# Causal attention with a recurrence behind it: from trips of 128 queries of two batches to trips of 64 queries of four

## The reference

```python
q, k, v = split(x @ c_attn_w + b)                       # heads of 32
k_img, v_img = cond @ uk_w.T + uk_b, cond @ uv_w.T + uv_b   # one key and value per batch
scores = q @ [k_img, k].T / sqrt(32)                    # [8, 16, 512, 513]
scores = where(key <= query + 1, scores, -10000) + mask
x1 = x + softmax(scores) @ [v_img, v] @ c_proj_w + b_proj
xw = x1 @ Wx + b_h
h_t = tanh(h_(t-1) @ Wh + xw_t)                         # t = 0 .. 511, h_(-1) = cond
out = x1 + h
```

## Time and profile before

| | |
|---|---|
| median of three runs | 1697.04 us (1691.76 to 1697.95) |
| profiled execution | 1689.44 us |
| its span | 1687.6 us |
| TensorE (PE) busy, of the span | 1521.2 us |
| setup, before the first unit's scores | 0 to 48 us |
| four blocks of attention | 48 to 246, 617, 1014 and 1425 us |
| tail, 128 steps | 1445 to 1678 us |

### The profile page before, as it was taken

One profiled execution on the slowest core, in us unless ns is written; L12 is line 12 of the kernel. 1 busy time (PEld: TensorE's weight loads), 2 busy tenths in 40 slices (PEclk: granted clock), 3 DMA queues, 4 the chain that ended last, 5 costly groups with the idle time before them and its releaser, 6 DMA issues.

```text
span 1687.6 us, 65682 instructions
## 1 busy us (share of the span) xinstructions
PE 1521.2 (90%) x28397; PEld 1288.2 (76%) x28397; DVE 817.9 (48%) x2592; ACT 718.4 (43%) x2289; POOL 369.9 (22%) x535
## 2 busy tenths in 40 slices
PE   6589988999999999999999988999999999777775
PEld 6478777778877878888888877888888788666664
DVE  4455554454545455555555545555565555222221
ACT  3355553444444444544445444454454545111111
POOL 2045552203131222203132130311313100000000
PEclk9799899999999999999999999999999999999999
DMA  7655555334344454445545445555555632000000
GB/s 252 184 186 179 166 181 145 111 96 124 106 126 116 120 145 132 129 110 144 143 137 151 112 136 148 142 156 133 151 140 156 165 89 70 9 15 10 15 9 15
DMA packets 139936, 204.73 MB, mean 121 GB/s; under 512 B 19432, under 2 KB 91240, under 8 KB 139136
## 3 DMA queue, kind: packets, MB, share of 16 engines
q1 hardware_dynamic: 112640, 128.05, 28.9%
q0 software_dynamic: 27008, 72.47, 13.0%
HBM read 133.06 MB, written 67.37 MB: 119 GB/s over the span
## 4 chain that ended last, share of the span: by engine, by line
PE 79%; DMA 6%; DVE 5%; issue 4%; ACT 4%; SPq 2%; POOL 0%; DVEq 0%; ACTq 0%; POOLq 0%
PE rec L1004 24%; PE turned L938 10%; PE dense L466 7%; PE dense L467 6%; PE dense L468 6%; PE rec L995 5%; PE scores L928 5%; PE pv L951 4%; PE scores L1004 4%; DMA xin<-x 3%; DVE pre L842 3%; ACT states L694 2%; PE pv L969 2%; DMA kq<-kq_dram 1%; PE dense L1011 1%
## 5 line engine op out<-in xcount | busy, mean ns | idle before, releaser
L1004 PE MATMUL rec<-wh,states 128*32 128x128 f32 x14336 | 485.2, 276 | 62.9 <-ACT states L694 61.3
L1004 PEld LDWEIGHTS rec<-wh,states 128*32 128x32 f32 x14336 | 376.0, 110 | 129.1 <-ACT states L694 90.7
L648 ACT ACTIVATE probs<-probs,nmax 128x128 f32<-128x128 f32 (+3 forms) x512 | 287.4, 562 | 209.5 <-DVE nmax L791 203.0
L694 ACT ACTIVATE states<-pre 128x32 f32<-128x32 f32 x512 | 133.3, 260 | 431.3 <-DVE pre L842 430.3
L842 DVE STREAM_TRANSPOSE pre<-rec 128x128 f32<-128x128 f32 x448 | 141.6, 316 | 342.1 <-PE rec L1004 338.9
L791 DVE CUSTOM_DVE_ANT_0 probs<-scores,msk,nimg 128x128 f32<-128x128 f32 (+3 forms) x512 | 276.2, 544 | 61.8 <-PE scores L928 54.5
L938 PE MATMUL turned<-ident,probs 128*128 128x128 f32 x1280 | 243.7, 290 | 13.1 <-ACT probsT L655 11.7
L928 PE MATMUL scores<-kq 96*128 96x128 f32 (+3 forms) x512 | 204.9, 403 | 18.5 <-DMA kq<-kq_dram 16.7
L938 PEld LDWEIGHTS turned<-ident,probs 128*128 128x128 f32 x1280 | 145.4, 141 | 78.8 <-issue 55.7
L800 DVE COPY probsT<-turned 128x128 f32<-128x128 f32 (+3 forms) x256 | 124.6, 487 | 80.1 <-PE turned L938 75.7
L655 ACT COPY probsT<-turned 128x128 f32<-128x128 f32 (+3 forms) x256 | 107.0, 418 | 95.8 <-PE turned L938 94.2
(11 more groups left out here) (159 smaller groups left out, 2218.6 us busy)
## 6 DMA issues: line engine op xcount, KB each, us to landing
kq<-kq_dram SPq DMA_DIRECT2D x96, 320.0 KB, 5.2
kq<-kq_dram SPq DMA_DIRECT2D x96, 256.0 KB, 4.4
kq<-kq_dram SPq DMA_DIRECT2D x96, 192.0 KB, 3.6
kq_dram<-qs_hi POOLq DMA_DIRECT2D x120, 128.0 KB, 2.9
kq_dram<-ks_hi POOLq DMA_DIRECT2D x120, 128.0 KB, 3.4
kq<-kq_dram SPq DMA_DIRECT2D x96, 128.0 KB, 2.8
xin<-x SPq DMA_DIRECT2D x32, 256.0 KB, 4.0
v_dram<-vbuf POOLq DMA_DIRECT2D x32, 256.0 KB, 3.1
```

Of the source, the lines that this page charges most:

```text
L648: act.activation(probs[:, g % PROBS, 0:n], probs[:, g % PROBS, 0:n], ACT.Exp, scale=-1.0, bias=nmax[:, e, h:h + 1], accum_out=rowsum[:, e, ...
L694: act.activation(state_cells(g), pre[:].rearrange("p f (b z) -> p f b z", z=GROUP)[:, :, :, s], ACT.Tanh).then_inc(h_ready, 1)
L1004: last = pe.matmul(rec_bank(g // GROUP)[Q * j:Q * j + Q, 0:P], state_tile(g - 1)[:, f, :], wh[:, f, P * j:P * j + P], start=False, stop=f ...
```

## The change

- **Trips**: 64 queries (`W`) of four batches (`QUADS` = 2 such trips a part, eight parts). Again 16 trips of 32 units of 128 query rows; a unit is now one head of two batches, rows 0 to 63 of the one and 64 to 127 of the other. A unit has `keys(g)` = 64, 128, ... 512 keys; 64 units of each size. Keys in tiles of 128 (`tiles_of`): 1, 1, 2, 2, 3, 3, 4, 4.
- **Scores**: float32, 32 rows of contraction, no split. Two matmuls a unit, each 32 rows by 64 columns of the array, one for each batch. The units u and u + 1 are written behind one another; their heads lie on neighbouring 32-row strips and their results in different PSUM banks. q stays in SBUF (`q`, two trips deep), k is stored once (one DMA a chunk) and loaded as one tile of 128 rows a group. The split's instructions are gone: ScalarE copies q, VectorE copies k.
- **Image scores** (L915, L917 before): four float32 matmuls a chunk with 64 columns of weights, where four fp32r ones with 128 were.
- **pv**: the same 32-column matmuls, with 64 columns moving in place of 128 and twice as many, since the two batches have different values. The last tile has 64 rows in every other part. Value tiles hold two batches; there are two in place of three.
- **Steps**: `FIRST` is 448. The 448 steps before it are spread by weight over everything from the end of part 0's last projection to the last trip's projection, and the tail has 64. `x1` holds two parts.
- **Sizes**: `PROBS` 5 for 4; other lags and the places of `begin` and of the chunks moved by a unit or two.

```diff
-FIRST = (BLOCKS - 1) * P
-PROBS = 4
+FIRST = S - W
+PROBS = 5
...
         if u < HEADS:
+            if u % 2 == 0:
+                emit([("score", v, 0, 0.07 + 0.107 * keys(g) / P) for v in (u, u + 1)])
             if u % HC == HC - 1:
                 loads += [("kqload", group, 0, 0.0) for group in range(GROUPS) if PLACES[group][0] == u // HC + 1]
-            emit([("score", u, 0, max(0.11, 0.053 * (block_of(g) + 1)) + 0.1)])
...
+    first, last = ends[QUADS - 1] + 1, begins[TRIPS - 1]
+    whole = sum(w for *_, w in main[first:last])
+    done, t = 0.0, 0
+    for at in range(first, last):
+        done += main[at][3]
+        while (t < FIRST and at > ends[(t // W + 1) * QUADS - 1]
+               and (done >= whole * (t + 0.5) / FIRST or at + 1 == last)):
+            place.setdefault(at, []).append(t)
+            t += 1
...
+        def store_keys(eng, g, i, stored):
+            p, r = divmod(g, QUADS)
+            eng.dma_start(k_dram[4 * r:4 * r + 4, i, :, W * p:W * p + W].rearrange("b p t -> p b t"),
+                          knew[:, i, :].rearrange("p (b t) -> p b t", b=4)).then_inc(stored, 16)
...
-                    for part in range(3):
-                        sp.dma_start(heads_tile(g)[Q * part:Q * part + Q].bitcast(F32),
-                                     kq_dram[part, r, :, c, e, 0:P + P * (p + 1)]
-                                     .rearrange("(j d) t -> d j t", d=Q)).then_inc(tile_loaded[g % LOADS], 16)
+                    sp.dma_start(heads_tile(g), k_dram[4 * r + 2 * e:4 * r + 2 * e + 2, c, :, 0:keys(trip)]
+                                 .rearrange("b p t -> p b t")).then_inc(tile_loaded[g % LOADS], 16)
...
-                    pe.matmul(scores[g % 2][:, 0:n], heads_tile(group)[0:3 * Q, j, 0:P],
-                              heads_tile(group)[0:3 * Q, j, P:P + n], start=True, stop=True).then_inc(scores_ready, 1)
+
+                    rows = slice(Q * j, Q * j + Q)
+                    for b in range(2):
+                        at = W * (2 * e + b)
+                        last = pe.matmul(scores[g % 2][W * b:W * b + W, 0:n], q[rows, trip % 2, c, at:at + W],
+                                         heads_tile(group)[rows, b, :], start=True, stop=True, skip_group_check=True)
+                    last.then_inc(scores_ready, 1)
...
-                    for k in range(p + 1):
-                        for j in range(HC):
-
-                            last = pe.matmul(pv[Q * j:Q * j + Q, P * c:P * c + P],
-                                             vtile[g % VTILES][:, k, Q * j:Q * j + Q],
-                                             probsT[:, (HC * g + j) % TURNED, P * k:P * k + P],
-                                             start=c == 0 and k == 0, stop=False, skip_group_check=True)
+                    for at in range(0, n, P):
+                        rows = slice(0, min(P, n - at))
+                        for b in range(2):
+                            mine = slice(at + W * b, at + W * b + W)
+                            for j in range(HC):
+
+                                last = pe.matmul(pv[Q * j:Q * j + Q, P * c + W * b:P * c + W * b + W],
+                                                 vtile[g % VTILES][rows, b, at // P, Q * j:Q * j + Q],
+                                                 probsT[rows, (HC * g + j) % TURNED, mine],
+                                                 start=c == 0 and b == 0 and at == 0, stop=False, skip_group_check=True)
```

More of the change, by code:

```diff
@@ L16 @@
 PAIRS = B // 2
-TRIPS = BLOCKS * PAIRS
+W = P // 2
+PARTS = S // W
+QUADS = 2
+PAIRED = 2
+TRIPS = PARTS * QUADS
 UNITS = 2 * H
@@ L20 @@
 GROUPS = HEADS // HC
-STEPS = S // (BLOCKS * PAIRS)
+STEPS = W // QUADS
 HALF = STEPS // 2
@@ L68, in block_of, with keys, tiles_of @@
 def block_of(g):
-    return g // PAIRS
+    return g // QUADS
+def keys(g):
+    return W * (block_of(g) + 1)
+def tiles_of(g):
+    return -(-keys(g) // P)
 def tile_places():
@@ L75, in tile_places @@
     for group in range(GROUPS):
-        size = HC * P * (block_of(group // 8) + 2)
+        size = 2 * keys(group // 8)
         if at + size > ROOM:
@@ L86, with v_loads @@
 PLACES = tile_places()
+def v_loads():
+    counts = []
+    for group in range(GROUPS):
+        n = keys(group // 8)
+        mine = 2 * (n // P > 0) + 2 * (n % P > 0)
+        counts.append(mine + (counts[group - VTILES] if group >= VTILES else 0))
+    return counts
+V_LOADS = v_loads()
 def main_order():
@@ L198, in put @@
         for name, lags in LAGS.items():
-            if kind in ("q", "k") and name == ("POOL" if g == 0 else "SP"):
+            if kind == "k" and name == ("POOL" if g == 0 else "SP"):
                 continue
@@ L554, in _ @@
         @block.gpsimd
         def _(pool):
-            for tile, a in ((ukb[:], uk_b), (bqk[:], b_qk), (causal[:], causal_in), (bproj[:], b_proj), (bx[:], b_h),
+            for tile, a in ((ukb[:], uk_b), (bqk[:], b_qk), (causal[0:W, :], causal_in[0:W, 0:W]), (causal[W:P, :], causal_in[W:P, W:P]),
+                            (bproj[:], b_proj), (bx[:], b_h),
                             (uvb, uv_b.rearrange("(a n) -> a n", a=1).broadcast_to([P, D])), (headmask, headmask_in),
@@ L936, in _ @@
                         pe.wait_ge(turned_copied[g % 2], g // 2)
-                    for k in range(p + 1):
-                        last = pe.transpose(turned[g % 2][:, P * k:P * k + P], probs[:, g % PROBS, P * k:P * k + P], ident[:])
+                    for at in range(0, n, P):
+                        last = pe.transpose(turned[g % 2][0:min(P, n - at), at:at + P],
+                                            probs[:, g % PROBS, at:min(at + P, n)], ident[:])
                     last.then_inc(turned_ready, 1)
                 elif kind == "pv":
-                    p = block_of(g // 8)
+                    n = keys(g // 8)
                     c = g % C
```

327 lines of the change are left out of this document (159 added, 168 removed).

## The result

The changed kernel takes 1743.44 us (median of 4 runs, 1736.61 to 1746.63), the kernel before beside it 1695.55 (4 runs): ratio 1.0279 [1.0239, 1.032], slower. The profiled execution took 1746.63 us.

The account below looks back on a forecast made before the run. The prediction took TensorE to bound the attention and the recurrence's own chain the tail. 1689.4 - 31 + 82 + 15 - 30 = 1725, plus 7.6 from profiled run to median, gave 1733 us; range 1664 to 1812.

Parts of the forecast that it names:

- Tail, -31: Recurrence: 64 steps leave the tail, 116 us less, and cost 85 us more in the attention; net -31 us.
- Scores, +82: Attention scores on TensorE: 201 us for 119, from 303 blocks (209 pairs together, 94 single units) in float32; +82 us.
- 0.09 to enter: TensorE's change of tile shape: entering one costs 0.09 us, read from a step behind the last dense matmul.
- pv, +15: Attention's pv matmuls: twice as many, half as wide, rounds near the array's own time; +15 us, near the lower end.
- the rival with its 1778: pv: matmuls never start closer than about 25 ns, so 128 us in place of 68; total 1778; no separate chance.
- Image scores, 0: Image scores on TensorE: as many matmuls in half the width; 0, some 10 us either way.
- Transposes, dense products and out, 0: Attention on TensorE: 1280 transposes before and after, 16 trips of 32 units as before; 0 us.
- Waits, -30: TensorE's idle in the attention (73 us) and lost clock (22 us): fewer, lighter transfers take back 30 us.
- serial strips: Scores: row strips run one after another, so joined pairs pay columns twice; 94 us more, 1827; chance 0.12.
- pv's bound: pv is bound by issue or weight loading: +73 us instead of +15, total 1791; chance 0.14.
- gap rival: TensorE's idle and lost clock in the attention, 111 us in all, go away; 1652, faster; chance 0.20.
- evening out: Scores' entries and exits cost today's 0.10 a matmul, 36 us less, and waits give 30; total 1697; chance 0.12.

Follow-up runs that it names:

- e3: Changed kernel with steps 384 to 447 taken out of the attention and run behind it, 128 tail steps again: 1776.64 us, ratio 1.0515 to the kernel before.
- e4: Changed kernel with scores written one unit at a time, so no two row strips can run at once: 1877.56 us, ratio 1.1111 to the kernel before.
- e1: Changed kernel with a step never put between the two units of a pair: 1715.71 us, ratio 1.015 to the kernel before.
- e8: Changed kernel with whole pairs, pv behind the transposes and steps anchored right ahead of pairs: 1711.71 us, ratio 1.0139 to the kernel before.
- e6: Changed kernel with second ScalarE and VectorE copies of q and k chunks put back as spent work: 1744.21 us, ratio 1.0337 to the kernel before.
- e10: Kernel before the change, with x's split and the next trip's chunks one unit later: 1661.13 us, ratio 0.9801 to the unedited kernel before.
- e2: Changed kernel with each pair of scores written ahead of pv and transposes, five probs buffers: 1780.07 us, ratio 1.0527 to the kernel before.
- e5: Changed kernel with pairs ahead of pv and transposes, six probs buffers and less key-tile room: 1729.27 us, ratio 1.0248 to the kernel before.

## Why the prediction was right, and where it was wrong

The direction and the time (1733 for 1743) held, and of the mechanism the row strips, the columns and the tail; that the time came so close is partly luck, since terms cancelled. Against the predicted +36 to the profiled time, the spans differ by +57. The scores' term was 38 us too low (with what its entries cost the transposes), and dense products and small kinds added 23 that I did not have; waits and setup gave 19 more than I took, tail, pv and image scores 21.

- **Tail, -31.** Steps and input parts with their idle made +77 - 84 - 30 = -37, and e3, which undoes it, costs 24 to 29. Right. The 64 steps stand 1.81 apart, as said.
- **Scores, +82.** Of its parts, "n x 1.667 ns" and "that all four matmuls of a pair run at once" are shown by e4. The 303 blocks are shown by e1, which won 35 us of scores with 47 fewer. The step that failed is "0.09 to enter": that was read behind a dense matmul, while most of the new entries stand behind transposes, where they cost 0.17. The kernel before enters a tiled stretch there 73 times, the changed kernel 369 times; 296 x 0.174 = 52 of the 55 us that the transposes took more. Measured: +64 in the scores and +55 in the transposes, +120. That the scores' own +64 lies near +82 is luck in part: the changed kernel's were put at 201 and took 203, but without any entry in them, as an entry is paid in the row ahead; the kernel before's were put at 119 and took 139, as a score ahead of a step pays 0.09 for the step's entry there too (some 10 us in all), and the first block ran at a granted clock of 0.89. The -17 for neighbouring steps mostly did not come, since a step beside a pair is a change of shape (e8).
- **pv, +15**, was +7. Two full key tiles take 0.56 by the median of 15 groups, near the 0.5 of the lower end and far from 0.9; with a last tile of 64 rows they take 0.72, the change of shape that the 7 us were for. 48 records take 0.78 to 0.94 above, 0.016 to 0.020 apart. So neither loading nor issue doubles a round. By the Trainium skill (TensorE: Matmul & The Clock Gate, "Wait — 56ns, not 53.3ns?") matmuls never start closer than about 25 ns. Each record taken as a matmul, as the prediction did, these rows disagree, and the rival with its 1778 falls. The trace of the kernel before denied it already, where the prediction has "neither shows nor denies": four records, one on each column tile, start within the 0.03 us from 705.66 to 705.69, and 0.0275 was an average over rounds:

```profile
705.66 0.32 PE L951 MATMUL pv<-probsT,vbuf 128*32 128x128 f32 x4
```

- **Image scores, 0**, were -7.
- **Transposes, dense products and out, 0.** The number of transposes did not change, but the dense products took 17 us more. Their place explains it. In the kernel before most runs of dense products stand behind a score, which is not tiled, and some 20 behind a tiled stretch; in the changed kernel 150 stand behind a tiled stretch, at 0.10 each, and 90 behind transposes or the like, at 0.08. That is 25 us for 9, and 25 more entries behind dense products at 0.09 are 2 more. Against e6 (395.2) the clock may count for some of the 7: e6 had 0.90 from 41 to 140 us, the changed kernel 0.79, but the kernel before had 0.84 there.
- **Waits, -30.** The idle in the attention fell by 42, the setup by 7. The ground that I gave, fewer and lighter transfers and the clock, was mostly wrong. The clock won nothing back in the profiled execution: 0.87 from 41 to 246 us, for 0.89 in the earlier trace rows. That execution is the slowest of its four, at a mean clock of 0.975 where the others had 0.979 to 0.984, so over the runs a few us may have come back. The waits of TensorE for `kq` and values (8.7 + 7.8 us behind the first scores) became 4.3, that is 12 of the 42. The largest part, 22.6, is waits of steps. On the kernel before e10 took away 16 of these by the later split of x, a line of the diff that I had passed over; that it is the same cause in the changed kernel is argued from the same lines and not shown, since the split was not moved back there.
- **"PROBS 5 is what pairs need"** holds for this order only. One place further ahead (e2) six are needed (e5).

Of the rivals, serial strips (1827) fall by e4 and pv's bound (1791) by its rows. The gap rival had 66 of 111 us to win; 42 came, none of them from the clock. The evening out at 1697 fails by the entry: it took 0.10 for entry and exit, and they are 0.26 to 0.35, with 0.06 to 0.10 more in what stands behind.

Open: what removed the part of the idle time that neither the transfers' waits nor the later split accounts for, and whether the split did in the changed kernel what it did in e10. Not run: the split moved back in the changed kernel; a placement that keeps the steps even and the entries few at once, and e10's placement with a part of the change.

## What to carry to other kernels

Count the changes of tile shape in the issue order, and price each by what stands before and behind it, since an operation that becomes dearer (here the transposes, +55 us) need not be one that was edited. Two matmuls on different row strips are one only while nothing comes between them, so a scheduler must treat them as one event. When one edit brings many small constants with it, try these alone on the old kernel first: here one of them, two places moved by a unit, was worth 2% there, inside a change that lost 3%.

## What the runs showed of the hardware that was not expected

- Entering a tiled stretch costs 0.09 us behind dense fp32r matmuls and 0.17 behind float32 transposes, in both kernels. Leaving one costs twice: 0.11 to 0.13 in a step whose successor has another shape, and then 0.06 in transposes or 0.10 in a dense product behind it.
- Four float32 matmuls of 448 columns, two row strips by two column halves, take the time of two on one strip: 0.91 against 0.90.
- 64-column float32 matmuls in 32-column tiles take 0.016 to 0.020 us a record on average, and four records on four column tiles start within 0.03 us.
- TensorE's granted clock over the setup differed between runs of the same work: 0.83 of 2.4 GHz in the changed kernel, a mixture of its two levels, and 1.00 in e6, each with the engine busy for 26 to 29 of 41 us.
